# An attention and FFN kernel on one core: where the six split operands of the FFN's products start in SBUF

## The reference

```python
x = x + xattn(ctx, layernorm(x), mask, mask, W_src, b_src, W_tgt, b_tgt, W_out, b_out)
h = layernorm(x)
h = silu((h @ w1.T) * s1) * ((h @ w2.T) * s2)   # w1, w2: 1024 x 256, entries -1, 0 or 1
h = gelu((h @ h1.T) * t1)                       # h1: 1024 x 1024, entries -1, 0 or 1
h = gelu((h @ h2.T) * t2)                       # h2: the same
x = x + (h @ w3.T) * s3                         # w3: 256 x 1024
```

## Time and profile before

| | |
|---|---|
| time, median of 2 runs | 907.39 us |
| lowest and highest | 907.35 and 907.44 us |
| span of the profiled execution, first to last instruction | 906.1 us |
| PE busy | 900.6 us, 7600 matmuls |
| DVE busy | 615.8 us |
| ACT busy | 390.9 us |
| granted TensorE clock | 1.000 |

### The profile page before, as it was taken

How to read it: one execution, slowest core, us unless ns; L and a number is a source line. 1 busy time by engine, 2 the same in 40 slices (tenths; PEclk the granted TensorE clock), 3 DMA queues, 4 the chain that set the end, 5 groups by cost and what they waited for, 6 DMA issues and landing times.

```text
span 906.1 us, 20825 instructions
## 1 busy us (share of the span) xinstructions
PE 900.6 (99%) x7600; PEld 865.1 (95%) x7600; DVE 615.8 (68%) x1224; ACT 390.9 (43%) x1100; POOL 76.9 (8%) x101
## 2 busy tenths in 40 slices
PE   9999999999999999999999999999999999999998
PEld 8899999999999999999999999999999999999998
DVE  5887858577585776857667586675857857576453
ACT  5872534435253252623525235253443524355231
POOL 3543000010000100001010010100001000000000
PEclk9999999999999999999999999999999999999999
DMA  9932132412314232142311424113241221303000
GB/s 350 382 114 58 60 88 69 122 52 78 84 46 122 58 98 64 40 122 69 112 45 35 122 69 122 35 50 106 69 122 46 72 84 59 94 24 106 24 13 14
DMA packets 82352, 79.27 MB, mean 87 GB/s; under 512 B 8592, under 2 KB 74896, under 8 KB 82320
## 3 DMA queue, kind: packets, MB, share of 16 engines
q1 hardware_dynamic: 81744, 78.31, 28.2%
q10 hardware_dynamic: 576, 0.52, 0.2%
HBM read 51.55 MB, written 27.26 MB: 87 GB/s over the span
## 4 chain that ended last, share of the span: by engine, by line
PE 96%; DVE 1%; DMA 1%; issue 0%; SPq 0%; POOL 0%; ACT 0%; DVEq 0%; POOLq 0%; ACTq 0%
PE F L627 56%; PE G L627 8%; PE F L740 7%; PE G L620 6%; PE G L478 6%; PE G L514 5%; PE G L496 2%; PE S L531 2%; PE G L603 2%; PE F L514 1%; PE S L467 1%; DMA cT<-ctx_t 0%; DMA p_dram<-pb 0%; DMA pr<-p_dram 0%; DVE pr L1107 0%
## 5 line engine op out<-in xcount | busy, mean ns | idle before, releaser
L863 ACT ACTIVATE g<-F,firsts 128x256 f32<-128x256 f32 x248 | 104.0, 472 | 322.9 <-PE F L627 322.7
L627 PE MATMUL F<-hBh,H 128*128 128x256 f32 x1008 | 239.2, 282 | 0.1
L627 PE MATMUL F<-hBl,H 128*128 128x256 f32 x1008 | 236.2, 279 | 0.0
L627 PE MATMUL F<-hAh,H 128*128 128x256 f32 x976 | 231.7, 282 | 0.0
L627 PE MATMUL F<-hAl,H 128*128 128x256 f32 x976 | 228.8, 279 | 0.0
L627 PEld LDWEIGHTS F<-hBl,H 128*128 128x128 f32 x1008 | 190.0, 189 | 0.4
L627 PEld LDWEIGHTS F<-hBh,H 128*128 128x128 f32 x1008 | 188.9, 187 | 0.6 <-ACT g L863 0.3
L627 PEld LDWEIGHTS F<-hAl,H 128*128 128x128 f32 x976 | 183.9, 188 | 0.3
L627 PEld LDWEIGHTS F<-hAh,H 128*128 128x128 f32 x976 | 183.0, 187 | 1.0 <-ACT sil L856 0.4
L1265 DVE CAST hBh<-g 128x512 fp32r<-128x512 f32 x64 | 28.4, 444 | 118.0 <-ACT g L863 117.8
L891 ACT ACTIVATE pr<-pr,nmx 128x128 f32<-128x128 f32 x240 | 92.7, 388 | 0.2
(11 more groups left out here) (160 smaller groups left out, 1520.0 us busy)
## 6 DMA issues: line engine op xcount, KB each, us to landing
p_dram<-pb SPq DMA_DIRECT2D x30, 512.0 KB, 3.3
pr<-p_dram SPq DMA_DIRECT2D x120, 128.0 KB, 3.2
H_raw<-h SPq DMA_DIRECT2D x16, 512.0 KB, 13.8
cT<-ctx_t SPq DMA_DIRECT2D x14, 512.0 KB, 3.6
x_dram<-xt SPq DMA_DIRECT2D x28, 256.0 KB, 2.4
out<-y SPq DMA_DIRECT2D x32, 128.0 KB, 1.7
x_in<-x_t SPq DMA_DIRECT2D x15, 256.0 KB, 2.7
x2T<-x_dram SPq DMA_DIRECT2D x60, 64.0 KB, 2.0
```

What stands on the lines that cost most here:

```text
L627: return mm(bank, W[0][:, k, cols], part[:, k, :], start=first, stop=last)
L863: fn(g[:, q % 2, m, :], mid_bank(f, q)[:, m, :], ACT.Gelu, scale=scols[:, col:col + 1]).then_inc(gelu_ready, 1)
```

## The change

The pad goes. Each of the six tensors is allocated 64 bytes (LINE = 16 elements) larger and starts at a multiple of 64; the view that the kernel uses begins `first` elements of 4 bytes behind that.

```diff
-PAD = 8
+LINE = 16
...
-        sb("pad", [P, PAD])
-        x2h, x2l = sb("x2h", [P, KD, T], F32R), sb("x2l", [P, KD, T], F32R)
-        hAh, hAl = sb("hAh", [P, KH, T], F32R), sb("hAl", [P, KH, T], F32R)
-        hBh, tile1_home = with_raw("hBh", KH, T)
-        hBl = sb("hBl", [P, KH, T], F32R)
+        def behind(home, first, k):
+
+            return home[:, first:first + k * T].rearrange("p (k t) -> p k t", k=k)
+
+        x2h, x2l = behind(sb("x2h", [P, KD * T + LINE], F32R), 0, KD), behind(sb("x2l", [P, KD * T + LINE], F32R), 6, KD)
+        hAh, hAl = behind(sb("hAh", [P, KH * T + LINE], F32R), 4, KH), behind(sb("hAl", [P, KH * T + LINE], F32R), 12, KH)
+        hBh_home, hBh_raw = with_raw("hBh", 1, KH * T + LINE)
+        hBh, tile1_home = behind(hBh_home[:, 0], 2, KH), behind(hBh_raw[:, 0], 2, KH)
+        hBl = behind(sb("hBl", [P, KH * T + LINE], F32R), 14, KH)
```

## The result

The changed kernel takes 914.64 us (914.47 to 914.82, 2 runs) against 907.39 before: a ratio of 1.008, with a 95% interval of 1.005 to 1.0109. It is slower by 7.3 us, within the 2% line and outside the noise. The profiled execution's span is 912.9 us against 906.1, so 6.8 us more.

The account below looks back on a forecast made before the run. The prediction took TensorE's matmul spacing as the bound; (a) gave plus 0.7 us and all other parts 0, so the median of 907.4 became 908.1, stated as 908 us, with a range of 880 to 935.

Parts of the forecast that it names:

- The bound: Whole kernel: TensorE busy 900.6 of 906.1 us, so time is a sum over matmuls; waits matter only if reaching PE.
- What the 8.9 ns are: Float32r matmuls at line 627: 116.7 ns against 107.8 for a float32 pass, put down to load and stream together.
- (a): x2h, read by 512 matmuls, goes from 32 to 0; taken to cost 0.7 us.
- (b): hAh and hAl as weights of line 740 go to 16 and 48; minus 0.7 to plus 0.7 us, taken as 0.
- (c): x2l, hA and hB as moving operands, 4608 matmuls, go to unseen starts; near bounds 6.5 us each way, taken as 0.
- the likeliest case: The forecast, with (c)'s near bounds and the case that nothing happens: 900 to 915 us, chance 0.45.
- (d): DVE and ACT writers at new starts: a cast up to 0.26 us longer hidden by 0.61 us of cover; taken as 0.
- (e): Load of tile 1's context into hBh's memory, now starting at 8: 1.7 us of cover; taken as 0.
- Faster: Rival: new starts keep PE's two read streams apart; 885 us with half the excess gone, 862 with all; chance 0.19.
- One more line: Rival: streams of x2l, hBh and hBl span one more 16-byte piece, 1.7 ns on 2560 matmuls; 912.4 us; chance 0.18.
- Slower by far: Rival: starts off a multiple of 16 upset the whole stream, 8.9 ns on 2560 matmuls; 931 us; chance 0.18.
- What I had named last: Sign of being wrong: matmul spacing that depends on how hi's start stands to lo's, since the two alternate; no size given.

Follow-up runs that it names:

- e8: Changed kernel with x2 and hA at 32, hB at 8, and the H1 and H2 products computing only 128 of 256 columns; 892.38 us.
- e5: Changed kernel with equal hi and lo starts in each pair: x2 at 0, hA at 40, hB at 48; 916.56 us.
- e11: Changed kernel with all six tensors starting at a multiple of 64 (0); 915.66 us.
- e12: Changed kernel with x2 and hA put back to 32, only hB's pair at 8 and 56; 920.55 us, 1.0137 times the kernel before.
- e6: Changed kernel with equal hi and lo starts in each pair: x2 at 8, hA at 24, hB at 16; 921.87 us.
- e2: Changed kernel with equal hi and lo starts in each pair: x2 at 24, hA at 8, hB at 56; 928.89 us.
- e3: Changed kernel with hi and lo starts x2 0 and 48, hA 8 and 56, hB 8 and 24; 916.0 us.
- e4: Changed kernel with only hB's pair put back to 32 and 32; 908.74 us, 1.0008 times the kernel before.
- e9: Kernel before plus one small matmul ahead of each product of H1 (96 columns) and H2 (40 columns); 912.67 us, 1.0054 times the kernel before.

## Why the prediction was right, and where not

*The bound.* Right: the time is a sum over matmul spacings, and the whole change of 6.8 us is a change of one spacing on 2048 matmuls; no wait reached PE.

*What the 8.9 ns are.* Half right. I read from the rows that neither a load (110 ns) nor a pass (107.8) needs 116.7 alone. e8 found 111.3 with half the columns, so only 5.4 ns of the spacing come with the full stream beside the load, not 8.9, and the floor is most likely the load's.

*(a)* x2h at 0, +0.7 us: it cost nothing here, x2 stayed at 1.87 us with x2l at 24. With both at 0 it took 1.90 (e5) and 1.89 us (e11), 1 to 2 ns a matmul more. So one moving operand at 0 doesn't cost the 1.4 ns between lines 740 and 627; whether two do was not separated from how the stage is entered.

*(b)* hA as stationary at 16 and 48, 0: right, 3.78 us.

*(c)* is the step that was mis-sized. I gave the unseen starts 0, with near bounds of 1.4 ns each way, taken from 0 against 32. Measured were 3.3 ns on hB's 2048 matmuls and nothing on hA's or x2's. The float32 rows that I leaned on were the wrong neighbours for a float32r stream: there a load has 215.6 ns to run in, which is probably why its meeting with the stream costs nothing. The time of 914.6 lies just within the likeliest case's own range of 900 to 915, and that is luck. The near bound was 1.4 ns on all 4608 matmuls, 6.5 us; what came was over twice that on fewer than half of them, 6.8 us. With only hB's pair changed, for which the same terms give less than for the whole, the time was 920.55 us (e12), beyond that range.

*(d), (e)* The writers and the early transfer, 0: right. The casts take 427 ns, and PE has no new wait for them.

*The rivals.* "Faster" did not come; no kernel with all of the work was faster than the one before, and no stretch of 128 with all its columns fell under 14.93 us. Only line 740's product gained, 3.74 us for 3.78 in e6 (3.75 in e2), 0.6 us in all. "One more line", at 912.4 the nearest in time, was wrong in its mechanism: it wanted 0.22 us on hB and a cost on x2l at 24, and there were 0.42 and none; e3's hB at 8 and 24, at 14.95 us in the loop, settles that it cannot be seen in the time. The rule from the Trainium skill, "SBUF — State Buffer", Specifications (TRN2), that each crossing to a new 16-byte line costs, did not show in these reads; a stream of 107.8 ns with 1.7 more would still be shorter than the step of 116.7, so the runs don't refute it. "Slower by far" wanted 8.9 ns on the same three operands; the 3.3 ns on hB and none on x2l, and e3's hB, speak against it. What I had named last, that hi's start and lo's might count together, came nearest: with 8 and 24 nothing in the loop, with 8 and 56 3.3 ns, though equal starts of 8 cost as well. That the way into a stage might count, no part of the prediction considered.

## What to carry to other kernels

Where TensorE is busy all the time, read the spacing of a long stretch (its length over its number) against the columns at the granted clock, and then against the load of the weights: here a float32r matmul of 256 columns with a load of its own runs at 116.7 ns, of which 111.3 stay when half the columns are taken away. Fewer loads may be worth more than any placing; that was not tried. Placing the operands cost up to 6.7 ns of 117 (e6), and it isn't a sum of parts: one part of this change alone cost 12.5 us, the whole 7.3. So a placing has to be measured as the whole program will run it, and one that was found by trial has to be tried again after any change to the stages around it.

## What the runs showed of the hardware that was not expected

- Halving the columns of a float32r matmul from 256 to 128 took its spacing only from 116.7 to 111.3 ns (e8).
- The same matmuls at the same addresses ran at 116.7 ns in one tile and 123.3 in the next (e6), and the wider spacing lasted through the stretch and through all tiles of the loop. In e4 it went from 116.8 to 120.0 in one tile near the end.
- One matmul of 96 columns ahead of a stretch of 128 moved the stretch's spacing from 116.7 to 117.8 ns; one of 40 columns ahead of another left it at 116.7 (e9).
- DVE's reads at 8 and at 32 behind a multiple of 64 took 287 and 288 ns; its casts took 427 ns with writes at 16 against 429 at 32 (hAh), and 445 at 8 against 444 at 32 (hBh).
